# Storing finished expert tiles straight to their tokens: indirect stores inside the loop and plain loads at the end, in place of 100 gathers

## What is computed

```python
rh = relu(features @ router_w1 + router_b1)
expert_logits = softmax(rh @ router_w2 + router_b2, axis=-1)
top_w, top_i = lax.top_k(expert_logits, 2)
routing_weights = softmax(top_w, axis=-1)
h1 = relu(einsum('bsd,edh->bseh', features, expert_w1) + expert_b1)
h2 = relu(einsum('bseh,ehf->bsef', h1, expert_w2) + expert_b2)
expert_out = einsum('bsef,efo->bseo', h2, expert_w3) + expert_b3
sel = take_along_axis(expert_out, top_i[:, :, :, None], axis=2)
combined = sum(sel * routing_weights[..., None], axis=2)
# features = layernorm(x); the result of the network is x + combined
```

## Time and profile before

| | us |
|---|---|
| median of three timed runs | 6405.18 |
| span of the profiled execution | 7249.7 |
| of it, routing, from 6500 to 6785 | 285 |
| expert loop, 6785 to 7094 | 309 |
| tail, 7094 to the end | 156 |

### The profile page before, as it was taken

The page is one execution under the profiler, slowest core; times in us unless marked ns, Lnnn a source line. Parts: engine busy times, 40 slices in busy tenths (PEclk is TensorE's granted clock), DMA queues, the critical chain, the costliest instruction groups (busy, mean ns, idle before and its releaser), DMA issues.

```text
span 7249.7 us, 87859 instructions
## 1 busy us (share of the span) xinstructions
PE 5328.2 (73%) x24977; PEld 4445.0 (61%) x24977; DVE 3382.5 (47%) x9891; ACT 1308.8 (18%) x2962; POOL 3860.9 (53%) x4349
## 2 busy tenths in 40 slices
PE   0111110667659999999899999979999899997794
PEld 0000000556537777777678887868788778876682
DVE  8511100666645555555464464436444554446323
ACT  0000000111101111111142242214111231111240
POOL 0777776000055555555888888830666326654205
PEclk9755555778779999999999999989999999999895
DMA  1000000221133333335310011021333223353223
GB/s 37 9 12 12 12 12 11 73 66 58 59 105 98 96 99 100 98 97 93 49 48 18 14 40 34 20 70 48 91 95 97 76 71 107 108 93 109 89 94 117
DMA packets 319771, 477.56 MB, mean 66 GB/s; under 512 B 99008, under 2 KB 240054, under 8 KB 319470
## 3 DMA queue, kind: packets, MB, share of 16 engines
q0 software_dynamic: 153136, 262.81, 14.8%
q1 hardware_dynamic: 166334, 211.17, 9.5%
HBM read 371.27 MB, written 102.33 MB: 65 GB/s over the span
## 4 chain that ended last, share of the span: by engine, by line
PE 57%; another core or an unknown queue 13%; DVE 11%; issue 11%; DMA 4%; DVEq 2%; ACT 1%; SPq 1%; POOL 1%; ACTq 0%; POOLq 0%
PE bank L2277 13%; PE bank L2288 13%; PE bank L2505 5%; PE bank L2338 5%; PE bank L2487 4%; PE bank L2323 4%; PE bank L2774 3%; PE bank L2630 2%; PE bank L2268 2%; PE bank L2816 1%; DMA sb_work_QT<-scratch_q 1%; DMA sb_rows<-scratch_xn,sb_row_of 1%; DMA sb_work_XC<-in_x 1%; DVE sb_STATE L1391 1%
## 5 line engine op out<-in xcount | busy, mean ns | idle before, releaser
L995 POOL DMA_INDIRECT sb_rows<-scratch_xn,sb_row_of x1760 | 1718.7, 977 | 1553.2 <-PE bank L2323 619.1
L988 POOL DMA_INDIRECT scratch_sorted<-sb_FREE x1564 | 1589.6, 1016 | 546.5 <-issue 379.2
L2288 PE MATMUL bank<-sb_work_FT,sb_W 128*128 128x250 f32 x4400 | 1006.9, 380 | 19.6 <-ACT sb_work_FT L1075 15.1
L2288 PEld LDWEIGHTS bank<-sb_work_FT,sb_W 128*128 128x128 f32 x4400 | 845.3, 193 | 134.6 <-ACT sb_work_FT L1075 22.0
L1075 ACT ACTIVATE sb_HT<-bank,sb_cols 128x250 f32<-128x250 f32 x1333 | 552.8, 467 | 2047.2 <-PE bank L2487 811.6
L2277 PE MATMUL bank<-sb_W,sb_HT 128*125 128x256 f32 x4000 | 894.2, 380 | 1.1 <-ACT sb_HT L1075 1.1
L2277 PEld LDWEIGHTS bank<-sb_W,sb_HT 128*125 128x125 f32 x4000 | 752.7, 188 | 115.4 <-ACT sb_HT L1075 1.9
L2277 PE MATMUL bank<-sb_W,sb_work_FT 128*125 128x256 f32 x1600 | 409.3, 406 | 449.8 <-issue 378.3
L2277 PEld LDWEIGHTS bank<-sb_W,sb_work_FT 128*125 128x125 f32 x1600 | 315.0, 201 | 518.0 <-issue 450.5
L2323 PE MATMUL bank<-sb_rows,sb_work_TM 128*125 128x257 f32 x1760 | 444.8, 392 | 91.2 <-issue 29.7
L1660 DVE TENSOR_TENSOR sb_FREE<-sb_FREE,bank 125x257 f32 x440 | 186.1, 423 | 698.0 <-PE bank L2323 455.1
(11 more groups left out here) (375 smaller groups left out, 7606.2 us busy)
## 6 DMA issues: line engine op xcount, KB each, us to landing
sb_rows<-scratch_xn,sb_row_of POOLq DMA_INDIRECT x1760
scratch_sorted<-sb_FREE POOLq DMA_INDIRECT x1564
scratch_qT<-sb_work_QF SPq DMA_DIRECT2D x100, 250.0 KB
sb_work_QF<-scratch_qT SPq DMA_DIRECT2D x100, 250.0 KB
sb_work_XC<-in_x SPq DMA_DIRECT2D x50, 250.0 KB
sb_work_ZT<-scratch_xn SPq DMA_DIRECT2D x50, 250.0 KB
sb_W<-in_L_mix_W SPq DMA_DIRECT2D x9, 1024.0 KB
sb_work_XC<-scratch_zs SPq DMA_DIRECT2D x28, 256.0 KB, 2.6
```

Of the source, the lines that this page charges most:

```text
L988: nc.gpsimd.indirect_dma_start(out=sorted_d[e], out_offset=bass.IndirectOffsetOnAxis(ap=pos[e][0:n, c:c + 1], axis=0), in_=rec[e][0:n, 2 * ...
L995: nc.gpsimd.indirect_dma_start(out=rows[:, t % RING, 0:D], out_offset=None, in_=table, in_offset=bass.IndirectOffsetOnAxis(ap=row_of[:, t: ...
L2288: ins = nc.tensor.matmul(dst[:, b, :], w[:, k0 + k, 128 * (b0 + b):128 * (b0 + b) + 128], source[:, k, :], start=(n == 0), stop=(n == 2 * ...
```

## The change

Rows of z get five more numbers (`DW` = 261): the token's row number, its two experts and their two shares. So a tile that is loaded for the loop brings with it whose rows it holds. In the loop DVE works out from these, with five small instructions a tile, the share of each row (`SHAREOF`) and its place in a new table `y_d` of 2 x 6250 rows (`OUT_AT`): the token's first choice goes to the first half, its second to the second half, padding to a place out of bounds, which isn't written. The eviction of the third layer adds the third bias on the way, ACT then scales the tile by the shares, and POOL stores it with two indirect stores of 128 rows. In the tail SP loads, for each chunk, the two halves of `y_d` with plain transfers, DVE adds each with one instruction, and SP stores the chunk. The gathers, the bias stage on PE and ACT and the index arithmetic (`place_results`, `place_gates`) are gone. `ZR` and `XB` lie in other buffers, and the six third biases are loaded to all 128 partitions.

```diff
-X_ACT = named(2, "turn") + named(1, "a") + named(0, "b")
-X_DVE = named(2, "w0", "bias") + named(1, "w1") + named(-1, "y")
+X_ACT = named(2, "turn") + named(1, "a") + named(0, "b") + named(-1, "y")
+X_DVE = named(2, "w0", "bias", "shares", "share", "tables", "table", "at") + named(1, "w1") + named(-1, "y")
...
-        zs_d = dram("zs", [NEXP1 * CAP, D])
-        ys_d = dram("ys", [NX * TILE, D])
+        zs_d = dram("zs", [NEXP1 * CAP, DW])
+        y_d = dram("y", [2 * N, D])
...
# SP
+                if j == NP - 4:
+                    sp.dma_start(bexp1, a["L1_ffn_expert_b3"].rearrange("(u e) n -> u e n", u=1)
+                                 .to_broadcast([128, NEXP1, D])).then_inc(weights_loaded["exp_rest"], 16)
...
-                    sp.dma_start(by_tile(ys_d)[:, t, :], YB[t % XRING].rearrange("p u n -> p (u n)"))\
-                        .then_inc(y_stored[t % XRING], 16)
...
+            for q in range(XRING):
+                sp.wait_ge(result_stored[q], 32 * ((NX - q + XRING - 1) // XRING))
+            for j in range(NC + YRING):
+                if j >= YRING:
+                    sp.wait_ge(result_added, 2 * (j - YRING + 1))
+                    n = 2 * (j - YRING)
+                    sp.dma_start(tiles(out)[:, n:n + 2, :], XM[:, n:n + 2, :]).then_inc(out_stored, 16)
+                if j < NC:
+                    for k in range(2):
+                        sp.dma_start(GY[j % YRING][:, k], tiles(y_d[k * N:(k + 1) * N, :])[:, 2 * j:2 * j + 2, :])\
+                            .then_inc(result_loaded[j % YRING], 16)
...
# POOL
-            for j in range(NC):
...
-                        nc.gpsimd.indirect_dma_start(
-                            out=GY[j % YRING][:, t, k, :], out_offset=None, in_=ys_d,
-                            in_offset=bass.IndirectOffsetOnAxis(ap=Y_AT[:, 2 * j + t, k:k + 1], axis=0))\
+            for t in range(NX):
+                q = t % XRING
+                wait(pool, x_dve.done("at", t))
+                wait(pool, x_act.done("y", t))
+                hold(pool)
+                for u in range(2):
+                    nc.gpsimd.indirect_dma_start(
+                        out=y_d, out_offset=bass.IndirectOffsetOnAxis(ap=OUT_AT[:, q, u:u + 1], axis=0),
+                        in_=YB[q][:, u, :], in_offset=None, bounds_check=2 * N - 1, oob_is_err=False)\
+                        .then_inc(result_stored[q], 16)
...
# ACT, at the end of turn b
+                t = b - 1
+                if t >= 0:
+                    wait(act, x_dve.done("y", t))
+                    for u in range(2):
+                        ins = move(YB[t % XRING][:, u, :], YB[t % XRING][:, u, :], scale=SHAREOF[:, t % XRING, u:u + 1])
...
# DVE, in body_c1
+                    nc.vector.tensor_copy(ZR[(j + 1) % ZN][:, 0:r, ROW:ROW + 1],
+                                          ROWID[:, ch:ch + r].rearrange("p (t u) -> p t u", u=1))\
...
# DVE, in turn b after w0 and the biases of tile t = b + 2
+                    q = t % XRING
+                    dve.wait_ge(tile_loaded[q], 16 * (t // XRING + 1))
+                    if t >= XRING:
+                        dve.wait_ge(result_stored[q], 32 * (t // XRING))
+                    nc.vector.scalar_tensor_tensor(SHARES[:, q], XB[q][:, :, OWNER:OWNER + 2], exp_all[:, t:t + 1],
+                                                   XB[q][:, :, SHARE:SHARE + 2], ALU.is_equal, ALU.mult)\
...
# DVE, the third layer's eviction, t = b - 1
-                    if t >= XRING:
-                        wait(dve, (y_stored[t % XRING], 16 * (t // XRING)))
-                    nc.vector.tensor_copy(YB[t % XRING], PSUMS[t % 2][:, :].rearrange("p (u n) -> p u n", u=2))\
+                    nc.vector.tensor_tensor(YB[t % XRING], PSUMS[t % 2][:, :].rearrange("p (u n) -> p u n", u=2),
+                                            bexp1[:, bass.ds(of_tile[t], 1), :].to_broadcast([128, 2, D]), ALU.add)\
...
# DVE, tail
-                        nc.vector.scalar_tensor_tensor(x, GY[j % YRING][0:T, t, k, :], GATE[:, 2 * j + t, k:k + 1], x,
-                                                       ALU.mult, ALU.add).then_inc(gate_added, 1)
+                    nc.vector.tensor_tensor(XM[:, 2 * j:2 * j + 2, :], XM[:, 2 * j:2 * j + 2, :], GY[j % YRING][:, k],
+                                            ALU.add).then_inc(result_added, 1)
```

More of the change, by code:

```diff
@@ L889, in _ @@
                 load_xn1(0, s)
-            load("exp_up", (bexp1, a["L1_ffn_expert_b3"]), *[expert(0, e) for e in range(NEXP1)])
-            sp.wait_ge(routing_cleared, 8)
+            load("exp_up", *[expert(0, e) for e in range(NEXP1)])
+            sp.wait_ge(routing_cleared, 11)
             for j in range(NP):
@@ L918, in _ @@
                 load_tile(t)
[L919 to L926, removed]
-                    sp.dma_start(by_tile(ys_d)[:, t, :], YB[t % XRING].rearrange("p u n -> p (u n)"))\
-                        .then_inc(y_stored[t % XRING], 16)
-            for j in range(NC):
-                sp.wait_ge(gate_added, 5 * (j + 1))
-                sp.dma_start(tiles(out)[:, 2 * j:2 * j + 2, :], XM[:, 2 * j:2 * j + 2, :]).then_inc(out_stored, 16)
+            for t in range(NX - XRING):
+                wait(sp, x_pe.done("turn", t))
+                wait(sp, x_dve.done("at", t))
+                load_tile(t + XRING)
+            for q in range(XRING):
[9 more added lines that the diff above has]
+                            .then_inc(result_loaded[j % YRING], 16)
             sp.wait_ge(out_stored, 16 * NC)
@@ L1274, in _ @@
                     relu_tile(b, "b", H2, PC, 1)
[L1276 to L1281, removed]
+                t = b - 1
[3 more added lines that the diff above has]
+                        ins = move(YB[t % XRING][:, u, :], YB[t % XRING][:, u, :], scale=SHAREOF[:, t % XRING, u:u + 1])
+                    ins.then_inc(*x_act.add("y", t))
         @block.vector
@@ L2173, in _ @@
             step("in_of", nc.vector.tensor_copy(in_of, tile_in))
[L2175 to L2191 removed]
+            step("exp_all", nc.vector.tensor_copy(exp_all, EXPERTS))
             biases = cols[:, col_at["exp1_b1"]:col_at["exp1_b1"] + 4 * NEXP1]\
@@ L2754, in _ @@
             wait(pe, route("done"))
-            nc.tensor.matmul(PSUMS[1][0:T, 192:192 + NEXP1], tilesT.to_broadcast([8, T]), lower[0:8, 0:NEXP1],
-                             start=True, stop=True)
-            nc.tensor.matmul(PSUMS[1][0:1, 64:64 + NX], ones[0:NEXP1, 0:1], ended, start=True, stop=True)
+            nc.tensor.matmul(PSUMS[1][:, 64:64 + NX], ones[0:NEXP1, :], ended, start=True, stop=True)
             nc.tensor.matmul(PSUMS[1][0:1, 128:128 + NX], tilesT[0:NEXP1, :], ended, start=True, stop=True)\
                 .then_inc(route_sums, 1)
-            wait(pe, route("in_of"))
-            pe.wait_ge(y_placed, 1)
+            wait(pe, route("exp_all"))
             for name in ("exp_up", "exp_rest"):
```

162 lines of the change are left out of this document (62 added, 100 removed).

## The result

The changed kernel takes 6530.44 us (median of four runs, 6526.52 to 6532.35). The kernel before took 6406.01 us beside it, so the ratio is 1.0193, with a 95% interval of 1.0178 to 1.0207: **124 us slower**. The forecast was 6545 us, between 6470 and 6640, slower.

What follows compares the result with a forecast made beforehand. PE was taken to bound the loop, POOL's gathers the tail. -156.2 + 104.5 + 5.5 + 175.5 + 2 = +131 us, taken as +140 for timed runs: 6405 + 140 = 6545 us, range 6470 to 6640.

Steps and rivals of the forecast that it cites:

- What goes: Old tail, from the last eviction to the end, removed as a whole: -156.2 us in the profile.
- The middle that I took: Sum between +131 us with the profiled old tail and +150 with a shorter one in timed runs: +140 us.
- The loop: Expert loop: a turn grows from 5.62 to 7.71 us over 50 turns, +104.5 us.
- the way round: Expert loop: scaling, POOL's start, two stores and landing, small instructions, weight copy and eviction in sequence, 7.71 us a turn.
- After the last eviction: Between loop and tail: scaling, wake-up, two stores and landing before a load may start, 5.5 us.
- The tail: New tail: 75 plain transfers, 19.2 MB at 112 GB/s on about five of sixteen engines, +175.5 us with its ends.
- Routing: Routing stage: DVE makes one more copy a pair, taken as +2 us.
- The second: Rival in the loop: stores come back in time and PE still bounds it, so +104.5 goes: 6440; chance 0.06.
- The third: Rival in the tail: plain transfers spread over sixteen engines at 386 GB/s, 6425 with the forecast loop; chance 0.05.
- The fourth: Rival for loop and tail: the change doesn't do what it says, both stay as before, 6405; chance 0.02.
- POOL's wake: Loop, from indices ready on DVE to the start of the waiting scatter on POOL: 0.91 us.
- the rule above: Plain transfers use the largest number of engines up to 16 dividing the slowest dimension: five for the tail's 125 partitions.

Runs made afterwards that it cites:

- e1: Changed kernel with the wait for stores moved to the eviction that reuses the buffer and eight places for the small numbers: 6435.45 us.
- e4: Changed kernel with three POOL memsets a tile between the wait for ACT's scaling and the two stores: 6579.99 us.
- e5: Changed kernel with the same three POOL memsets a tile placed ahead of both waits: 6537.45 us.
- e2: Changed kernel with each load and store of the tail cut into 112 and 13 partitions: 6439.82 us.
- e6: Changed kernel with both the wait moved to the eviction and the tail's transfers cut at 112 partitions: 6345.61 us.
- e0_before: The kernel before, unchanged, timed and profiled once more: 6405.8 us, profiled span 6410.0.
- e7: Changed kernel with the wait moved, the tail cut at 112 partitions and the output's stores issued by ACT instead of SP: 6342.03 us.

## Why the prediction was right

- **What goes.** The first profile's tail was 156.2 us and I estimated 138 for the timed runs. The new profile has 139.8, so 138 was the better of the two. The middle that I took counts 147 for it, which makes the difference 7 us too small.
- **The loop: right in its place and nearly in its size.** Forecast 7.71 us a turn and +104.5, measured 7.56 and +96.4. Leg by leg, forecast against the rows above: scaling with its start 0.89 against 0.95; POOL's start 0.91 against 0.81; two stores and landing 3.67 against 3.78; small instructions 1.02 against 1.00; weight copy 0.48 against 0.34; eviction 0.74 against 0.68. No leg is off by more than 0.14, although none of these instructions stood in the trace of before: the nearest rows (7 and 8 for the stores) priced them. e1 shows that the way round was the cause, e4 that the turn grows with a leg of it, e5 that POOL's load doesn't count. One sign came out otherwise: PE is busy 79% of the loop (305 of 389 us) and not 73%. The same matmuls record 305 us here and 292 before; why, no run here separates.
- **After the last eviction** 5.5 forecast, 5.9 measured.
- **The tail: right in its cause, 13 us too long.** 175.5 forecast, 162.3 measured. The mis-sized term is the rate: I took 112 GB/s for 19.2 MB, and the tail runs at 120 to 121, which makes 159 us. The last fourteen slices of the earlier trace rows stand at 116 to 123, so the upper end was the one to take: 156 + 4.5 = 160.5. The ends come to some 3 us instead of 4.5, of which the 1.5 for the first data had no row behind it.
- **Routing**, +2 forecast: not to be seen. The zero rows land 4.2 us earlier after than before, within the scatter of some 20 us just named. What the edits in that stage cost by themselves stays open.
- **Sum.** +96.4 + 168.2 - 139.8 = +125 against +140 forecast and +124.4 timed. Too high were the loop (8 us), the new tail (13) and routing (2); the old tail, taken 7 too long, took part of that back. Without that the sum would have been 23 us too high.
- **The range.** It doesn't come out of the bounds that it names: loop and tail at their bounds together, with the middle for the old tail, give 6510 to 6659 and not 6475 to 6640. The measured 6530 lies inside both.
- **The rivals.** The second (stores come back in time) is what e1 builds: 6435.45 measured, 6440 forecast. The third (transfers over sixteen engines) is what e2 builds: 6439.82 measured, 6425 forecast at 386 GB/s; the transfers reached 265. Its border, a turn of 7.30 with 73 us of transfers and 4.5 us of ends, stood at +13 us, 0.2%; e2 is at +34.6. Between them lie 50 x 0.26 = 13 us of turn and 16 us of old tail that the timed runs don't have, less 5 us, since e2's 72.8 include its ends: +37. Neither rival alone would have made the change pay; both together do (e6). The fourth (no change) is outside the interval of the ratio.
- The Trainium skill, on the page named above under "Issuing engine by pattern", calls the plain path generally the faster one. Here 100 indirect gathers, their sums and the output's stores took 137.8 us from the last tile store's landing (6272.2 in e0_before) to the end, and 75 plain transfers 162.3; cut so that all engines take part these took 73. The sentence holds here once the shape fits.

## What to carry to other kernels

When results are handed to a slower way out, put the wait for it directly ahead of the instruction that reuses the buffer, not among the instructions that prepare a later tile: here a ring of four places had one turn of slack, and moving the wait gave back the whole 97 us. Sum the way round leg by leg and compare it with the engine that bounds the loop; here a way of 7.6 us in a loop of 5.6, with one turn for it, cost the difference in each turn, though no engine was near its limit. And look at the DMA share of a stream of plain transfers before sizing it: here 0.33 that didn't move meant that a third of the engines worked, and a cut at a multiple of sixteen partitions more than halved the stage.

## What the runs showed of the hardware

- **Start of an indirect store.** POOL starts a memset 0.10 us after ACT's scaling ends (e4), but an indirect store 0.80 to 0.81 us after it, with POOL idle before it for 5.2 us (after), 4.0 (e5) or 3.3 (e1). Right behind memsets a store starts after 0.36 (e4), right behind another store after 0.30. So what the prediction called POOL's wake is not a wake of POOL at large: it is the start of an indirect store behind a standstill. Where the 0.45 to 0.5 us go when POOL was just at work, no run here separates.
- **Five engines and sixteen.** With the counts of the rule above, five engines moved 120 GB/s, 24 each; sixteen moved 265 with one issuer and 302 with two, 17 to 19 each, all in runs of 1024 bytes. Three times the engines gave 2.2 to 2.5 times the rate.
- **A DMA share of 0.86 left room.** With one issuer the slices stood mostly at 8 and 9 tenths, 0.86 over the stage (e6), and yet a second issuer, on ACT, raised the share to 0.95 and the rate from 261 to 302 GB/s (e7).
